# Orders of steps in a four-layer network on one core: the state space scan and the second attention

## The reference, cut to what matters

```python
scores = jnp.einsum('bhsd,bhtd->bhst', q, k) * scale      # causal
attn = jnp.einsum('bhst,bhtd->bhsd', softmax(scores), v)
out = (g * attn).transpose(0, 2, 1, 3).reshape(b, sl, H * D) @ Wo.T
```

```python
a = exp(dt * -exp(A_log));  db = dt * x * B               # per head and token
states = associative_scan(a, db)                          # state = a * state + db
y = einsum(states, C) + D * x;  y = y * silu(z)
y = y * rsqrt(mean(y*y over the 256 channels of a group) + 1e-5) * norm_w
out = y @ W_out + b_out
```

## Time and profile before

| | us |
|---|---|
| median of 3 runs (3261.70 to 3263.66) | 3263.38 |
| the profiled execution | 3263.04 |
| its span, by the profile | 3261.3 |
| PE busy | 2835.9 (87%) |
| DVE busy | 1789.4 (55%) |
| ACT busy | 903.9 (28%) |
| POOL busy | 743.9 (23%) |

### The profile page before, as it was taken

How to read it: one execution, slowest core, us unless ns; L and a number is a source line. 1 busy time by engine, 2 the same in 40 slices (tenths; PEclk the granted TensorE clock), 3 DMA queues, 4 the chain that set the end, 5 groups by cost and what they waited for, 6 DMA issues and landing times. The chain is left out here.

```text
span 3261.3 us, 34764 instructions
## 1 busy us (share of the span) xinstructions
PE 2835.9 (87%) x13440; PEld 1743.0 (53%) x13440; DVE 1789.4 (55%) x3527; ACT 903.9 (28%) x1609; POOL 743.9 (23%) x809
## 2 busy tenths in 40 slices
PE   5888889989999999999899946988878888687997
PEld 3556555654554554555555533555545555565665
DVE  5565561227657656566552246777756777434223
ACT  2434451113333333232231112222222222222222
POOL 3221210013223222222210011333323233433003
PEclk8999999989999999999999967999989999888998
DMA  4113111030000000000001000000000000024223
GB/s 130 29 32 53 28 39 52 1 127 1 1 1 1 1 1 1 1 1 1 14 1 62 1 26 13 10 14 11 7 10 14 14 11 25 16 93 173 62 65 95
DMA packets 53362, 100.60 MB, mean 31 GB/s; under 512 B 10128, under 2 KB 34832, under 8 KB 52048
## 3 DMA queue, kind: packets, MB, share of 16 engines
q1 hardware_dynamic: 49608, 88.94, 9.6%
q0 software_dynamic: 3072, 8.39, 0.8%
q10 hardware_dynamic: 520, 1.07, 0.2%
HBM read 54.32 MB, written 18.61 MB: 22 GB/s over the span
## 5 line engine op out<-in xcount | busy, mean ns | idle before, releaser
L1180 ACT ACTIVATE back<-ps,front 128x128 f32<-128x128 f32 (+7 forms) x256 | 189.5, 740 | 617.7 <-DVE front L1222 617.6
L1145 PE MATMUL ps<-back 128*128 128x512 f32 x576 | 296.4, 610 | 67.2 <-DVE back L1241 34.1
L825 DVE TENSOR_REDUCE front<-ps 128x1 f32<-128x512 f32 (+3 forms) x384 | 197.4, 552 | 112.3 <-PE ps L681 85.8
L1794 DVE TENSOR_TENSOR_SCAN back<-ps,back 128x512 f32<-128x512 f32 x128 | 155.5, 1216 | 128.8 <-PE ps L1645 128.8
L1269 POOL TENSOR_SCALAR back<-back,front 128x128 f32<-128x128 f32 (+5 forms) x192 | 143.0, 746 | 325.3 <-DVE front L1231 322.8
L1222 DVE TENSOR_REDUCE front<-ps 128x1 f32<-128x128 f32 (+7 forms) x256 | 194.0, 758 | 8.8
L786 ACT ACTIVATE back<-ps 128x1024 f32<-128x1024 f32 (+1 forms) x192 | 149.4, 808 | 137.3 <-PE ps L703 136.3
L1633 PE MATMUL ps<-front 128*128 128x512 f32 x320 | 160.4, 642 | 29.9 <-ACT back L1736 13.7
L1136 PEld LDWEIGHTS ps<-front,back 128*128 128x128 f32 x1152 | 136.6, 141 | 83.8 <-issue 61.9
L1136 PE MATMUL ps<-front,back 128*128 128x128 f32 x1152 | 163.5, 274 | 4.6 <-DVE back L1213 4.6
L1145 PEld LDWEIGHTS ps<-back 128*128 128x128 f32 x576 | 93.6, 190 | 137.1 <-ACT back L1186 55.5
(11 more groups left out here) (306 smaller groups left out, 5466.6 us busy)
## 6 DMA issues: line engine op xcount, KB each, us to landing
whole<-l_w SPq DMA_DIRECT2D x32, 512.0 KB, 14.3
front<-back SPq DMA_DIRECT2D x128, 64.0 KB, 2.0
rounded<-rounded SPq DMA_DIRECT2D x120, 64.0 KB
rounded<-front SPq DMA_DIRECT2D x120, 64.0 KB
xg<-front SPq DMA_DIRECT2D x1, 6016.0 KB, 32.4
front<-xg SPq DMA_DIRECT2D x47, 128.0 KB, 2.1
yg<-front SPq DMA_DIRECT2D x47, 128.0 KB, 1.7
front<-l_win SPq DMA_DIRECT2D x1, 4640.0 KB, 13.3
```

Of the source, the lines that this page charges most:

```text
L825: e.tensor_reduce(self.nm[u % 2][:, r, t, h:h + 1], self.bank(step)[:, 0:n], AX.X, ALU.max, negate=True).then_inc(D.sem, 1)
L1145: e.matmul(PS[:, 7, :], self.V[:, j, G % 4 * 128:G % 4 * 128 + 128], self.turned(("turn", n, j)), start=(j == 0), stop=(j == qt)).then_inc ...
L1180: e.activation(self.P[n % 2][:, h, :nk], s[:, :nk], ACT.Exp, bias=st[:, 0, h:h + 1], scale=1.0, accum_out=st[:, 1, h:h + 1]).then_inc(A.se ...
L1794: e.tensor_tensor_scan(m.LT[:, h, four, :].rearrange("p a b -> p (a b)"), self.bank(step, self.B), m.ident4, 0.0, ALU.mult, ALU.add).then_ ...
```

## The change

In Heads1 the steps are laid out on slots, eight in a unit (two for each head). `score` of head h stands in slot 2h, `turn` j of unit n in slot 8n + 10 + 8j // (qt + 1), the `mul` of it two slots later, `proj` and `out` at places from a table. The steps of DVE, POOL and ACT now have names of their own (`rope`, `max`, `exp`, `sum`, `o`), so they can stand elsewhere in the list than the matmul before them: `end` of a head stands ahead of `max` of the next one, `exp` behind the turns of both its slots, `rope` and `sum` behind `exp`. All turns are copied by ACT.

In MambaScan each engine has an order of its own: a table AT gives each step a place in units of halves relative to n, and `order(engine)` sorts by it. Tiles 16 and 18 (then 17 and 19) are made by quads of groups, the first pair at the start, the others at places 7, 15 and 23. `bt` is four transposes into one bank, with two banks for a quad instead of eight for a batch. C*B is copied to SBUF by ACT (`CB`), DVE multiplies it into three of four heads, POOL into the fourth. `var` is read by ACT instead of DVE; `out` is scaled by ACT into a buffer O (four of 128x256 per half) and added to x by POOL (two of 128x512 per half). W12 is loaded after the last `cb`. Some buffers move.

```diff
-        rest, now, end = [], [], None
+        for n, (G, qt) in enumerate(units):
+            for j in range(qt + 1):
+                slot = 8 * n + 10 + 8 * j // (qt + 1)
+                turn[slot] = ("turn", n, j)
+                mul[slot + 2] = ("mul", n, j)
...
+            for i in range(4):
+                put(G + 1, *((1, 2), (1, 3), (2, 0), (2, 1))[i], ("out", G, 2 * i))
+            for h, (qt, at) in zip(range(-1, 4), ((1, 0), (2, 0), (2, 1), (3, 0), (3, 1))):
+                put(G, qt, at, ("proj", G, 1, h))
+            for h, (qt, at) in zip(range(-1, 4), ((5, 0), (5, 2), (6, 0), (6, 2), (7, 0))):
+                if G < 7:
+                    put(G, qt, at, ("proj", G + 1, 0, h))
...
+                        if 0 <= m < 64:
+                            order.add("end", m, k)
+                        if n < 64:
+                            order.add("max", n, h)
+                    elif n < 64:
+                        order.add("exp", n, h)
+                for s in late:
+                    order.add(*s)
...
-        i = 4 * n + h - (4 if q < 16 else 3 if q == 16 else 2)
+        i = 4 * n + h - (2 if q == 0 or q > 16 else 3 if q in (1, 2, 16) else 4)
```

```diff
+    AT = {
+        "pe": {"raw": (-2.5, -2), "scan": (-1.1, -1, -0.8, -0.6), "xd": (-0.75, -0.6), "cp": (-0.2,),
+             "cb": (-0.55,), "st": (0.05,), "y": (0.25, 0.3, 0.6, 0.8), "gate": (0.15, 0.3), "var": (1.45,),
+             "out": (1.85, 2.2)},
+        "act": {"raw": (-2.45, -2), "silu": (-1.4, -1.2), "cb": (-0.5,), "gate": (0.15, 0.35),
+             "square": (1.05, 1.1), "mean": (1.45,), "out": (1.95, 2.2)},
+        "dve": {"tap1": (-1.8, -1.7), "tap2": (-1.8, -1.5), "tap3": (-1.8, -1.4),
+             "scan": (-1, -0.8, -0.65, -0.5), "xd": (-0.65, -0.4), "cp": (-0.25,), "bd": (-0.4,), "cb": (-0.4,),
+             "h": (0.2, 0.3, 0.3, 0.5), "end": (0.65, 0.7)},
+        "pool": {"raw": (-2.45, -2.2), "sel": (-1.1,), "cb": (-0.5,), "gate": (0.55, 0.6), "square": (1.15,),
+             "mean": (1.42,), "out": (1.85, 2.35)},
+    }
...
+        for q in range(4):
+            t = (8 * q, .0) if q == 0 else (8 * q, -1.0)
+            conv += [(t, q // 2, 16 + q % 2, 0), (t, q // 2, 18 + q % 2, 1)]
+        for u in range(16):
+            conv += [((2 * u, 0.0), u // 8, 2 * (u % 8) + s, s) for s in range(2)]
...
-                t = m.LT[:, :, four, :].rearrange("p h a b -> p h (a b)")
-                e.tensor_tensor(t, t, self.bank(step, self.B).unsqueeze(1).broadcast_to([128, 4, 512]),
-                                ALU.mult).then_inc(D.sem, 1)
+                t = m.LT[:, 0:3, four, :].rearrange("p h a b -> p h (a b)")
+                e.tensor_tensor(t, t, m.CB.unsqueeze(1).broadcast_to([128, 3, 512]), ALU.mult).then_inc(D.sem, 1)
...
-                    t = e.scalar_tensor_tensor(x, p[:, j * 256:j * 256 + 256],
-                                               m.rs[n % 2][:, 2 * (i + j):2 * (i + j) + 1], x, ALU.mult, ALU.add)
+                    t = e.activation(m.O[r][:, j * 256:j * 256 + 256], p[:, j * 256:j * 256 + 256], ACT.Copy,
+                                     scale=m.rs[n % 2][:, 2 * (2 * r + j):2 * (2 * r + j) + 1])
...
+                e.tensor_tensor(x, x, m.O[step[2]], ALU.add).then_inc(G.sem, 1)
```

More of the change, by code:

```diff
@@ L949, in plan, with put @@
         units = self.units = [(G, qt) for G in range(8) for qt in range(8)]
[L951 to L961, removed]
+        turn, mul, beside = {}, {}, {}
+        for n, (G, qt) in enumerate(units):
[3 more added lines that the diff above has]
+                mul[slot + 2] = ("mul", n, j)
+        def put(G, qt, h, *steps):
+            beside.setdefault(8 * (8 * G + qt) + 2 * h, []).extend(steps)
+        for G in range(8):
+            for i in range(4):
[5 more added lines that the diff above has]
+                    put(G, qt, at, ("proj", G + 1, 0, h))
+        put(4, 1, 2, *[("v", 1, i) for i in range(8)])
         order.add("gate")
@@ L965, in plan @@
             order.add("v", 0, i)
-        for s in make(0, 0, (-1, 0, 1, 2, 3)):
-            order.add(*s)
-        rest, now, end = [], [], None
-        for n, (G, qt) in enumerate(units):
-            for h in range(4):
[L971 to L987, removed]
@@ L988, in plan @@
-        order.add(*end)
-        for s in rest + now + [("out", 7, i) for i in (0, 2, 4, 6)]:
-            order.add(*s)
+        for h in range(-1, 4):
+            order.add("proj", 0, 0, h)
+            order.add("rope", 0, 0, h)
+        held = None
+        for n in range(67):
+            for h in range(4):
+                late = []
+                for half in range(2):
+                    slot = 8 * n + 2 * h + half
+                    if half == 0:
+                        if n < 64:
+                            order.add("score", n, h)
+                        for s in beside.get(slot, ()):
+                            order.add(*s)
+                            if s[0] == "proj":
+                                late.append(("rope",) + s[1:])
+                            if s[0] == "out":
+                                late.append(("sum",) + s[1:])
+                                if s[2] == 6 and held:
+                                    order.add(*held)
+                                    held = None
+                    if slot in turn:
+                        order.add(*turn[slot])
+                    if slot in mul:
+                        order.add(*mul[slot])
+                        _, m, j = mul[slot]
+                        if (m % 8, m // 8 > 0) == (0, True):
+                            held = ("o", m)
+                        elif j == units[m][1]:
+                            order.add("o", m)
+                    if half == 0:
+                        m, k = (n, h - 1) if h else (n - 1, 3)
+                        if 0 <= m < 64:
+                            order.add("end", m, k)
+                        if n < 64:
+                            order.add("max", n, h)
+                    elif n < 64:
+                        order.add("exp", n, h)
+                for s in late:
+                    order.add(*s)
@@ L1532, in __init__ @@
+        self.orders = {"pe": p, "act": a, "dve": d, "pool": g}
+        self.raws = [s[1:3] for s in p if s[0] == "raw" and s[3] == 0]
+        self.raw = {r: i for i, r in enumerate(self.raws)}
+        self.pn, self.an, self.dn, self.gn = [{s: i + 1 for i, s in enumerate(o)} for o in (p, a, d, g)]
         ring_a, ring_b = Slots(2), Slots(3)
         self.slot = {}
-        for step in order.steps:
-            kind = step[0]
-            if kind == "raw":
-                for tt in range(2):
-                    self.slot[step + (tt,)] = ring_a.take("a", step + (tt,))
-                    p.add(*step, tt)
-                    a.add(*step, tt)
-            elif kind == "first":
-                g.add(*step)
-            elif kind == "tap":
-                d.add(*step)
-                if step[3] == 3:
-                    a.add("conv", *step[1:3])
-            elif kind == "bt":
+        for step in p:
+            if step[0] in ("raw", "gate", "var", "out"):
+                self.slot[step] = ring_a.take("a", ("mean", step[1]) if step[0] == "var" else step)
+            elif step[0] in ("bt", "cb"):
```

477 lines of the change are left out of this document (232 added, 245 removed).

## The result

The changed kernel took 3045.68 us (median of 4 runs, 3045.56 to 3046.93), the kernel before 3263.52 on the same chip: ratio 0.933, 95% interval 0.931 to 0.935, 217.8 us less. The forecast was 3055, with a range of 3018 to 3120. The profiled execution has a span of 3044.0 us.

A forecast was written before the change was run, and what follows sets the result against it. PE was taken to bound both stages, with idle time. Scan 37 + 647 + 16.5 = 700 us instead of 847 (147 less) and attention 60 less make 207 off 3263.04: 3056, stated as 3055, 80% range 3018 to 3120.

The forecast's parts named there:

- Bound: Attention and scan: PE bounds both, with 80.7 us idle in the attention and 131 us in the scan.
- 66.1 us of `mul` waits gone: Attention: `mul` two slots behind its turn hides the copy, so its 66.1 us of waits in 71 gaps go.
- `end` ahead of `max` costs 20 us: Attention: the lengthened chain on DVE and ACT costs PE 2.5 us per G in five-block units, 20 us in eight.
- ACT's load: Attention: ACT takes over DVE's copies of turns, 84 us more, from 321.7 to 406 us, no bound.
- Scan, PE's work: Scan: PE has 20.1 us of work per half at full clock, 640 us in all 32.
- Scan, overhead of 5.5%: Steady scan: 5.5% for remaining waits, stalls and slow clock, making 613 us of PE work 647 us.
- Start at 37 us: Scan's start: the first `y` comes at 37 us instead of 71, 34 us earlier.
- DVE 500, POOL 359, ACT 273: Scan: busy times move to DVE 500 us from 578.6, POOL 359 from 237, ACT 273 from 199.
- rivals 2 and 3: Scan: shared interface makes DVE the bound, 3092 us, chance 0.13; DVE and POOL take turns, 3276 us, chance 0.03.
- Tail 16.5 us: Scan's end: POOL's sum of 1.27 us behind ACT's copy makes it 16.5 us instead of 15.
- 1, waits moved from `mul` to `score`: Attention: it gains nothing worth naming, as waits move to `score` and `turn`; 3106 us, chance 0.10.
- 4, a wait overlooked: Scan halves: one overlooked wait of 1.5 us per half loses 46 us of the gain; 3102 us, chance 0.12.

The follow-up runs named there:

- attn_old_list_copies_on_act: The changed kernel's scan with the old attention in its old list, but all copies of turns on ACT: attention 1040.0 us (1016.6 before), ratio 0.955.
- scan_bc_all_at_start: The changed kernel with all four B and C tiles of the first batch made at the start, not two: scan 673.9 us against 670.6, ratio 0.933.
- the single list: The changed kernel with the scan's new division of work in the old one list for all engines, B and C as before: scan 855.4 us, ratio 0.985.

## Why the prediction was right, and where not

The total was 9 us off, but that is luck in part: by the forecast's own measures the scan came out 27 us better than 700, the attention 13 worse than 60 off, and `v` started 4.7 us later for a reason outside the change. The mechanism was right for the scan and for the waits of `mul`; one step in the attention was not.

- *Bound.* Right for both stages: PE, with idle time made by the order. attn_old_list_copies_on_act shows that `mul` waited for its place, not for DVE.
- *66.1 us of `mul` waits gone.* Right as the slots' effect; with `max` first 0.4 are left beside ACT's copies. 25.3 remained through the next step, where I had said under 15. From the first `proj` to the last `mul` it is 938 us; 920 were expected, and over 960 would have been wrong.
- *`end` ahead of `max` costs 20 us.* This is the step that failed: it costs 49.9. I had found the chain and looked for it in the unit with five blocks alone, where it is even with PE as computed (2.4 us). For what the units with two to four blocks bring into it I set 2 us of lateness, since `rope` hides the exponential. It hides that, but lengthens DVE's row: in a head with rope the row is 4.30 us by itself. The chain alone costs 28.3 us, not far from my 20. What I had at nothing is the gate product's wait for POOL: my 0.19 us was its mean before (187 ns, 24 of 256 of them slowed by a rope sum), and in the new order 75 of 256 meet such a sum and the mean is 428 ns. That is 22.0 us by its experiment. The wait of `score` for `exp` at five blocks came as I had said. Attention: 47 instead of 60 us off.
- *ACT's load.* 84 us more expected, to 406; it is 406.67.
- *Scan, PE's work.* 20.1 us per half expected; from `st` to `st` it is 20.07 over 29 halves.
- *Scan, overhead of 5.5%.* Mis-sized: 613 us of work took 616.3 from the first `y` to the last (2565.5 - 1949.2), half a per cent. That gives 31 us; the start took 5 back and the tail gave 2. The waits of `y` and `out` went, and with them the slow clock from the first `y` to the last but for 3.4 us at its beginning, as forecast.
- *Start at 37 us.* It was 42.2; PE waits there 3.8, 4.5 and 2.7 us for silu, DVE's scan and `cp`, one after another. What I counted as a gain of the quads was none for the first batch (scan_bc_all_at_start).
- *DVE 500, POOL 359, ACT 273.* DVE 536.5, POOL 420.7, ACT 272.5. Contention cost DVE less than I said and POOL more. Taps rose from 1.36 and 1.41 us to 1.59 and 1.61, 26 us over 120 taps and so 1.3 us for the six of a half, where I had 2.8 for eight operations. For POOL I had set nothing: its sums of `out` take 1.60 instead of 1.27 and its quarter of `cb` 2.72, 68 us in all. None of it reached PE, and rivals 2 and 3 did not come true. I had cited "GPSIMD Engine Reference", section "Key points", of the Trainium skill for contention between POOL and a DVE instruction with two SBUF inputs. The trace agrees (taps of up to 2.29 us against 1.26); the one instruction for which it cost time was the gate product in the attention (1.14 us against 0.16), where I had not applied it.
- *Tail 16.5 us.* From the last `y` to the end of the last sum into x it is 14.7 us, and it was 15.3 before: POOL's sum behind ACT's copy made the tail no longer. (To the next stage's first DVE operation it is 19.2, and 19.8 before.)
- *Rivals.* 1, waits moved from `mul` to `score`, came for 10.9 us. 4, a wait overlooked, took place in a milder form, but in the attention, not in the scan.

## To carry to other kernels

In a list kept in order, a step that waits for another engine belongs behind all steps that don't: here `end`, which waits for the exponential, behind `max`, which does not, worth 50 us of 970. Where PE waits is not where the lateness arises; with banks to run ahead on, look one or two units earlier, at the engine whose row has no gaps. A new division of work pays only when the order lets it: here the move of `mean` and `out` was worth 40 us with an order for each engine, and a whole new division nothing in one list. And a change of order also changes who runs beside whom: the gate product became slow without a change to it.

## What the runs showed of the hardware

A DVE instruction of 128x1 with two SBUF inputs took up to 1.15 us when POOL had just started a two-input sum of 128x512, against 0.16 otherwise. In the changed kernel this holds without exception: 75 of the 256 gate products took longer than 0.3 us, each began during such a sum, and 180 with nothing on POOL took 158 to 161 ns. (The last one began 0.09 us before a sum's end.) POOL's operation need not have two inputs: with `max` first, seven products took 0.51 to 0.53 us that began 0.1 us into POOL's scaling of k (L1282), which reads one tensor. The same product with one tensor input and the other factor as scalar pointer took 212 to 216 ns in all 256 cases, 76 of them begun during a POOL sum. It is slower by 0.05 us alone, and doesn't wait.

The wait goes both ways. POOL's head of `cb` and DVE's three heads, in the changed kernel, start and duration:
```profile
2335.67 2.70 POOL L1912 TENSOR_TENSOR back<-back,front 128x512 f32<-128x512 f32 x1
```
```profile
2335.49 1.76 DVE L1856 TENSOR_TENSOR back<-back,front 128x1536 f32<-128x1536 f32 x1 [0.60 <-ACT front L1763]
```
DVE began 0.18 us earlier and took its usual 1.76; POOL's 1.27 became 2.70, ending 1.12 us after DVE. All 32 pairs of this kernel are so: DVE first, DVE at 1.76, POOL at 2.63 us or more. In the single list the pair meets in either order. There 27 of DVE's 32 products were slow, up to 2.88 us, and each began during a POOL operation; 11 of POOL's 32 were slow, up to 2.85, and each began during DVE's product, while the 21 that began with DVE idle took their 1.26 to 1.27. So in these traces whichever starts second waits. DVE operations that read one input from PSUM, such as its running product, did not slow POOL: 28 sums of `out` that began during one took 1.27 us.
